# Six blocks of the last round sorted by pair of experts and run as 17 listed steps in place of 24

## The reference

```python
for r in range(R):                                # R = 4 rounds
    flat = cur.reshape(-1, h)
    logits = flat @ Wg[r] + bg[r]
    vals, idx = jax.lax.top_k(logits, TOPK)       # TOPK = 2 of E = 4
    w = jax.nn.softmax(vals, axis=-1)
    cw = jnp.sum(jax.nn.one_hot(idx, E, dtype=flat.dtype) * w[..., None], axis=1)
    hmid = jax.nn.gelu(jnp.einsum('nh,ehf->enf', flat, W1) + b1[:, None, :])
    y = jnp.einsum('enf,efh->enh', hmid, W2) + b2[:, None, :]
    cur = cur + jnp.einsum('ne,enh->nh', cw, y).reshape(b, s, h)
...
xn = _layernorm(x)
x = x + mixer(xn) * _silu(experts(xn))
```

## Time and profile before

| what | us |
|---|---|
| median of three runs | 784.72 |
| lowest and highest | 784.56, 784.82 |
| span of the profiled execution | 782.9 |
| TensorE busy in it | 777.2 |
| VectorE busy | 689.3 |
| ScalarE busy | 641.1 |
| GpSimd busy | 115.2 |

### The profile page before, as it was taken

One profiled execution on the slowest core, in us unless ns is written; L12 is line 12 of the kernel. 1 busy time (PEld: TensorE's weight loads), 2 busy tenths in 40 slices (PEclk: granted clock), 3 DMA queues, 4 the chain that ended last, 5 costly groups with the idle time before them and its releaser, 6 DMA issues.

```text
span 782.9 us, 9951 instructions
## 1 busy us (share of the span) xinstructions
PE 777.2 (99%) x3392; PEld 619.2 (79%) x3392; DVE 689.3 (88%) x1096; ACT 641.1 (82%) x873; POOL 115.2 (15%) x141
## 2 busy tenths in 40 slices
PE   8999999999999999999999999999999999999998
PEld 6778788887888878888788887888877788888887
DVE  7999987899888889879899788987988989988998
ACT  7989888787888877888788877887877878888886
POOL 0122111111111111111111111111111111111110
PEclk9999999999999999999999999999999999999999
DMA  8467572332642416333154322643227434655453
GB/s 267 139 132 182 128 208 50 95 95 41 148 89 62 107 28 163 92 64 88 33 157 107 81 57 41 149 108 96 41 41 175 108 56 107 134 123 122 70 117 71
DMA packets 77010, 81.62 MB, mean 104 GB/s; under 512 B 48800, under 2 KB 54688, under 8 KB 72992
## 3 DMA queue, kind: packets, MB, share of 16 engines
q0 software_dynamic: 18624, 34.61, 25.8%
q1 hardware_dynamic: 57920, 46.11, 19.5%
q10 hardware_dynamic: 416, 0.26, 0.1%
HBM read 41.91 MB, written 3.93 MB: 59 GB/s over the span
## 4 chain that ended last, share of the span: by engine, by line
PE 95%; ACT 2%; DVE 2%; issue 0%; DMA 0%; DVEq 0%
PE h_bank L1079 15%; PE h_bank L1080 15%; PE h_bank L1083 15%; PE y_bank L1152 15%; PE y_bank L1142 15%; PE y_bank L1140 14%; PE p_bank L1079 2%; PE p_bank L1083 2%; PE p_bank L1080 2%; PE r_bank L1189 1%; ACT g L465 1%; ACT g_hi L471 1%; DVE g_lo L759 0%; DMA cur<-in_x 0%; DVE stats L600 0%
## 5 line engine op out<-in xcount | busy, mean ns | idle before, releaser
L465 ACT ACTIVATE g<-h_bank,b_c 128x512 f32<-128x512 f32 x512 | 329.3, 682 | 77.8 <-PE h_bank L1083 77.0
L759 DVE TENSOR_TENSOR g_lo<-g,g_hi 128x1024 fp32r<-128x1024 f32 x256 | 310.0, 1222 | 72.8 <-ACT g_hi L471 71.2
L471 ACT ACTIVATE g_hi<-g 128x1024 fp32r<-128x1024 f32 x256 | 271.8, 1062 | 8.1
L415 POOL DMA_DIRECT2D cur<-tmp x126 | 110.6, 878 | 642.4 <-DVE tmp L773 544.1
L1079 PE MATMUL h_bank<-cur_hi,w_hi 128*128 128x512 f32 x512 | 202.9, 396 | 0.2 <-ACT cur_hi L513 0.2
L1083 PE MATMUL h_bank<-cur_lo,w_hi 128*128 128x512 f32 x512 | 202.2, 395 | 0.0
L1080 PE MATMUL h_bank<-cur_hi,w_lo 128*128 128x512 f32 x512 | 202.1, 395 | 0.0
L1140 PE MATMUL y_bank<-g_hi,w_hi 128*128 128x512 f32 x504 | 196.2, 393 | 0.0
L1142 PE MATMUL y_bank<-g_hi,w_lo 128*128 128x512 f32 x488 | 193.6, 397 | 0.0
L1152 PE MATMUL y_bank<-g_lo,w_hi 128*128 128x512 f32 x504 | 137.9, 395 | 0.1
L1079 PEld LDWEIGHTS h_bank<-cur_hi,w_hi 128*128 128x128 f32 x512 | 96.2, 188 | 26.6 <-issue 3.8
(11 more groups left out here) (153 smaller groups left out, 410.5 us busy)
## 6 DMA issues: line engine op xcount, KB each, us to landing
cur<-tmp POOLq DMA_DIRECT2D x126, 256.0 KB, 3.3
cw_b<-cw_scratch SPq DMA_DIRECT2D x31, 1024.0 KB, 5.2
xn_t<-cur SPq DMA_DIRECT2D x8, 256.0 KB, 3.1
cur<-in_x SPq DMA_DIRECT2D x7, 256.0 KB, 5.0
xr<-in_x SPq DMA_DIRECT2D x28, 64.0 KB, 3.4
out<-o SPq DMA_DIRECT2D x28, 64.0 KB, 2.1
xn_scratch<-o POOLq DMA_DIRECT2D x6, 256.0 KB, 3.0
xr<-xn_scratch SPq DMA_DIRECT2D x24, 64.0 KB, 2.5
```

Of the source, the lines that this page charges most:

```text
L415: pool.dma_start(cur[:, block_of(s // E)], tmp[:, s % SUMS, :], accum_op=ALU.add).then_inc(summed, DMA)
L465: nc.scalar.activation(g[:, gb, ft * BLK:(ft + 1) * BLK], hb[ft][:, :], ACT.Gelu_apprx_tanh, bias=b1_c[:, e * FT + ft:e * FT + ft + 1]).th ...
L471: nc.scalar.activation(g_hi[:, gb, h], g[:, gb, h], ACT.Copy).then_inc(g_hi_done, 1)
L759: nc.vector.tensor_tensor(g_lo[:, gb, h], g[:, gb, h], as_f32(g_hi[:, gb, h]), ALU.subtract).then_inc(g_lo_done, 1)
```

## The change

The last round is done otherwise for blocks 0 to 5. The two best experts of their 3072 tokens are found ahead of time, the tokens are sorted by their pair of experts (six pairs, in an order in which neighbours share an expert), and the sorted tokens are cut into six blocks again. A sorted block then needs only the experts of the pairs that lie in it. A list of block and expert is made on the chip; it always has 17 entries, and each is run as one step (an item) with its block, weights, bias and gate read through registers. If fewer are needed, the rest of the 17 run with a gate of zeros. Steps 0 to 95 are rounds 0 to 2, steps 96 to 99 block 6, steps 100 to 116 the items, steps 117 to 120 block 7. So there are 121 steps.

Around that:

- TensorE turns each of the six blocks to rows of tokens (`turn_row`, four transposes), counts the pairs (`count_pairs`), turns the sorted rows back (`turn_back`), turns the gates, and after the items turns each block to rows (`turn_end`). All of these go through the one bank `r_bank`, in a fixed order (`BANK_JOBS`).
- GpSimd scatters the rows to their places in `sorted_rows` (4 indirect DMAs for a block), gathers the mixer's result and x of the sorted tokens (4 for a block), and scatters the output rows (4 for a block).
- SyncE copies the expert's weights of each item from SBUF to SBUF into one of three places `staged` (two copies of 512 KB for an item), with bias and gate.
- VectorE finds pairs and places, makes the list (`list_items`, 20 small instructions), and multiplies and adds at the end (`silu_product`, `finish_rows`). For the sorted blocks these stand in place of the former end stages.
- The mixers of blocks 0 to 6 start every 11 steps instead of every 14, with 13 stages each; the projection of R moves into the stage of `mixer_values`, and the inverse root into that of `mixer_squares`. The last mixer runs in steps 102 to 114.
- `g_lo` lies in the same memory as `g`.

```diff
@@ -13,9 +13,13 @@
 TPB = BLK // D
 RP = 32
 RT = BLK // RP
-TURNS = R * NB
-STEPS = TURNS * E
-PASSES = TURNS // 2
+
+SORTED = 6
+ITEMS = 2 * SORTED + 5
+TURNS = R * NB - SORTED
+FIRST_ITEM = E * (TURNS - 1)
+LAST_AT = FIRST_ITEM + ITEMS
+STEPS = LAST_AT + E
 GRP, GW = 16, 8
 LN_EPS = 1e-5
...
-MIX_FROM, MIX_EVERY = 15, 14
-END_FROM = STEPS - E * NB + E
+MIX_AT = (15, 26, 37, 48, 59, 70, 81, 102)
+STAGES, PLACES = 13, 3
...
-JOB_AT = {0: J_W, 1: J_A, 2: J_K, 3: J_V, 5: J_R, 6: J_G, 12: J_S}
+JOB_AT = {0: J_W, 1: J_A, 2: J_K, 3: J_V, 4: J_R, 5: J_G, 10: J_S}
...
+def items_through(j):
+    return min(2 * j + 7, ITEMS)
...
+SORT_LOGITS_AT = {0: 80, 1: 89}
+COUNTS_AT = 89
+ROW_END, ROW_MID = {0: 84, 1: 85, 2: 86, 3: 91, 4: 92}, {5: 94}
+BACK_END, BACK_MID = {0: 97, 3: 99, 5: 100}, {1: 98, 2: 99, 4: 100}
+SILU_AT = {j: FIRST_ITEM + items_through(j) + 1 for j in range(SORTED)}
+GATHER_AFTER = {0: 103, 1: 108, 2: 105, 3: 110, 4: 112, 5: 114}
...
+        def unit_of_w1(i):
+            return max(2 * i - 1, 0)
+
+        def unit_of_w2(i):
+            return min(2 * i + 2, 2 * ITEMS - 1)
+
+        def place_free(engine, v):
+
+            u = v - PLACES
+            if u < 0:
+                return
+            if u == 2 * ITEMS - 1:
+                engine.wait_ge(down_done, LAST_AT)
+            elif u == 0 or u % 2 == 1:
+                engine.wait_ge(up_done, FT * (FIRST_ITEM + (u + 1) // 2 + 1))
+            else:
+                engine.wait_ge(down_done, FIRST_ITEM + (u - 2) // 2 + 1)
...
-                if k >= 2:
+                if k == TURNS - 1:
+                    sp.wait_ge(combined, 2 + FIRST_ITEM)
+                    sp.wait_ge(row_stored[2], DMA * TPB)
+                elif k >= 2:
...
+            def stage(v, src):
+
+                place_free(sp, v)
+                sp.dma_start(as_f32(staged[:, v % PLACES, :, :]), as_f32(src)).then_inc(stage_full[v % PLACES], DMA)
+
+            def stage_w1(i):
+                stage(unit_of_w1(i), w1_all[:, bass.ds(experts[i], 1), :, :].rearrange("p a n f -> p (a n) f"))
...
+                q = i % ITEM_PLACES
+                sp.wait_ge(combined, 2 + max(FIRST_ITEM - E, FIRST_ITEM + i - ITEM_PLACES + 1))
+                sp.dma_start(gate_item[:, q, :],
+                             sorted_gates[bass.ds(gate_rows[i], 1), :].rearrange("a c -> (a c)").partition_broadcast(128)).then_inc(gate_full[q], DMA)
...
+            def load_rows(j):
+
+                q = j % IN_PLACES
+                if j == 0:
+                    for n in range(OUT_PLACES):
+                        sp.wait_ge(row_sent[n], DMA * TPB * SORTED // OUT_PLACES)
+                if j >= IN_PLACES:
+                    sp.wait_ge(r_empty, bank_job("back", j - IN_PLACES) + 1)
+                    sp.wait_ge(tok_back, j - IN_PLACES + 1)
+                sp.dma_start(rows_in[:, q, :, :],
+                             sorted_rows[j * BLK:(j + 1) * BLK, :].rearrange("(t p) c -> p t c", p=128)).then_inc(row_back[q], DMA)
...
+
+            sp.wait_ge(listed, 1)
+            sp.wait_ge(b2_beside, 1)
+            regs = [sp.alloc_register(f"expert{n}") for n in range(ITEMS)]
...
+            stage_w1(0)
+            load_bias(0)
+            load_rows(0)
+            load_rows(1)
+            stage_w1(1)
+            load_bias(1)
...
+            load_rows(4)
+            stage_w2(1)
+            load_gate(1)
+            load_rows(5)
...
+            for i in range(3, ITEMS):
+                if i + 1 < ITEMS:
+                    stage_w1(i + 1)
+                    load_bias(i + 1)
+                stage_w2(i)
+                load_gate(i)
+                if i == 6:
+                    store(NB - 2)
+                    load_x_again(NB - 1)
+                elif i == ITEMS - 2:
+                    spread_gates(TURNS - 1)
...
+            def scatter_rows(j):
+
+                q = j % OUT_PLACES
+                pool.wait_ge(row_ready, j + 1)
+                pool.wait_ge(place_ready, 1)
+                for t in range(TPB):
+                    pool.indirect_dma_start(out=sorted_rows,
+                                            out_offset=bass.IndirectOffsetOnAxis(ap=place_i[:, j * TPB + t:j * TPB + t + 1], axis=0),
+                                            in_=rows_out[:, q, t, :], in_offset=None,
+                                            bounds_check=SORTED * BLK - 1).then_inc(row_sent[q], DMA)
...
+                else:
+                    pool.wait_ge(row_stored[j - 3], DMA * TPB)
+                for t in range(TPB):
+                    c = j * TPB + t
+                    pool.indirect_dma_start(out=s_and_x[j][:, t, :], out_offset=None, in_=sx_rows,
+                                            in_offset=bass.IndirectOffsetOnAxis(ap=id_i[:, c:c + 1], axis=0),
+                                            bounds_check=SORTED * BLK - 1).then_inc(sx_loaded[j], DMA)
+
+            def scatter_out(j):
+
+                pool.wait_ge(row_out, j + 1)
+                for t in range(TPB):
+                    c = j * TPB + t
+                    pool.indirect_dma_start(out=out, out_offset=bass.IndirectOffsetOnAxis(ap=id_i[:, c:c + 1], axis=0),
+                                            in_=s_and_x[j][:, t, 0:D], in_offset=None,
+                                            bounds_check=SORTED * BLK - 1).then_inc(row_stored[j], DMA)
...
+                else:
+                    pool.dma_start(cur[:, block_of(turn_of(s))], tmp[:, s % SUMS, :], accum_op=ALU.add).then_inc(summed, DMA)
+                if COUNTS_AT <= s < COUNTS_AT + SORTED:
+                    scatter_rows(s - COUNTS_AT)
+                for j in at_step(SILU_AT, s - 1):
+                    scatter_out(j)
+                for j in at_step(GATHER_AFTER, s):
+                    gather_sx(j)
...
+            def pair_tokens(half):
+
+                cols = COLS // 2
+                h = slice(half * cols, (half + 1) * cols)
+                rank_experts(bank_job("sort_logits", half), 128, cols, R - 1)
+                link(nc.vector.tensor_scalar(picked[:, h, :], rank[:, 0:cols * E].rearrange("p (t e) -> p t e", e=E), 1.5, None, ALU.is_lt))
+                for c, (a, b) in enumerate(PAIRS):
+                    last = nc.vector.tensor_tensor(pair[:, c, h], picked[:, h, a], picked[:, h, b], ALU.mult)
+                last.then_inc(pairs_set, 1)
+                score_experts(128, cols)
+
...
+            def silu_product(j):
+
+                dve.wait_ge(silu_th, j + 1)
+                nc.vector.scalar_tensor_tensor(out=silu, in0=silu, scalar=1.0, in1=cur[:, block_at(j)],
+                                               op0=ALU.add, op1=ALU.mult).then_inc(silu_ready, 1)
+
+            def finish_rows(j):
+
+                job, s_part, x_part = bank_job("end", j), s_and_x[j][:, :, 0:D], s_and_x[j][:, :, D:2 * D]
+                dve.wait_ge(sx_loaded[j], DMA * TPB)
+                dve.wait_ge(r_full, job + 1)
+                nc.vector.scalar_tensor_tensor(out=s_part, in0=rb[:, :].rearrange("p (t d) -> p t d", t=TPB), scalar=0.5, in1=s_part,
+                                               op0=ALU.mult, op1=ALU.mult).then_inc(r_empty, 1)
+                dve.wait_ge(r_empty, job + 1)
+                nc.vector.tensor_tensor(s_part, s_part, x_part, ALU.add).then_inc(row_out, 1)
...
+                        for j in at_step(SILU_AT, s - 1):
+                            finish_rows(j)
...
+                if s == COUNTS_AT:
+                    token_places()
+                elif s == BACK_END[5] + 1:
+                    token_ids()
+                for j in at_step(SILU_AT, s):
+                    silu_product(j)
...
+            def up_item(s1):
+
+                i = s1 - FIRST_ITEM
+                v, block = unit_of_w1(i), newest_block(i)
+                if i == 0:
+                    pe.wait_ge(listed, 1)
+                    regs = [pe.alloc_register(f"slot{n}") for n in range(ITEMS)]
+                    pe.load(regs, tables[0:1, T_SLOT, :])
+                    slots.extend(pe.snap(reg, donate=True, min_val=0, max_val=SPLITS - 1) for reg in regs)
+                hi, lo = (ap[:, bass.ds(slots[i], 1), :].rearrange("p a c -> p (a c)") for ap in (cur_hi, cur_lo))
+                w_hi, w_lo = w1_of(s1)
+                pe.wait_ge(stage_full[v % PLACES], DMA * (v // PLACES + 1))
+                pe.wait_ge(sorted_split, 2 * block + 1)
+                for ft in range(FT):
+                    pe.wait_ge(gelu_done, FT * (s1 - 1) + ft + 1)
+                    w = slice(ft * D, (ft + 1) * D)
+                    mm_high(hb[ft][:, :], w_hi[:, w], w_lo[:, w], hi)
+                    if ft == 0:
+                        pe.wait_ge(sorted_split, 2 * block + 2)
+                    mm_low(hb[ft][:, :], w_hi[:, w], lo).then_inc(up_done, 1)
...
+            def count_pairs():
+
+                pe.wait_ge(r_empty, bank_job("counts", 0))
+                pe.wait_ge(consts_made, 1)
+                pe.wait_ge(pairs_set, 2)
```

(18 more changed lines are left out.)

713 lines of the change are left out of this document (544 added, 169 removed).

## The result

The changed kernel takes **803.3 us** (median; 803.0 to 804.1), the kernel before 784.7 in the same comparison: 1.024 times as long, 95% interval 1.0225 to 1.0254. So it is slower by 2.4%, where 772 and faster was forecast. The profiled execution has a span of 801.3, against 782.9.

The account below looks back on a forecast made before the run. TensorE, busy 99% of the span, was taken as the bound: 28.6 us less work, less the waits, gave -12.3 against 782.9, so 770.6, and 772 with the 1.8 around it; range 764 to 780, chance 0.60.

Parts of the forecast that it names:

- Sum: -28.6 + 7.1 + 0.5 + 2.7 + 1.0 + 5.0: TensorE's work, VectorE's lateness, `turn_back(0)`, `turn_back(5)`, register load and last item's weights, in us: -12.3 in all.
- VectorE, steps 47, 82, 106: VectorE's carried-over work makes TensorE wait 0.5, 1.0 and 0.2 us in these steps.
- `count_pairs`: Step 89: squares, root, `g_lo` and ranking on VectorE make `pair` late; TensorE waits 3.0 us.
- `silu_product` at `turn_end`: Near step 110: VectorE delivers the product late for `turn_end`; one wait of 2.4 us.
- `turn_back(0)`: End of step 97: sorted rows arrive after scatters and SyncE's register loads; nothing to 2.6 us, taken as 0.5.
- `turn_back(5)`: Step 100: `load_rows(5)` stands behind `stage_w2(1)` on SyncE's queue; wait of 2.7 us (0 to 4).
- registers, first item: TensorE's register load ahead of the first item costs 1.0 us, taken from a round trip of 1.7.
- end of SyncE's queue: Step 116: `stage_w2(16)` comes behind `spread_gates(25)` and its 1 MB, so `down(116)` waits 5.0 us (2 to 8).
- step 110: VectorE's squares, root, a split and carry 3.3 make `silu_product` late for `turn_end`: 2.4 us.
- Register loads cost by the register: Rival: at 0.21 us each, 3.6 on TensorE and 2.1 more at `turn_back(0)`: 777 us; chance 0.12.
- GpSimd becomes the bound: Rival: indirect DMAs of 1.7 us delay steps 89 to 94 and 108 to 115: 791.5 us; chance 0.06.
- The third rival: Copies of weights come late in each item, steps 100 to 116, 14 waits of 0.9: 785 us; chance 0.07.

Follow-up runs that it names:

- a_fill: The changed kernel with TensorE given transposes of the identity to do in seven of its long waits; 803.9 us.
- a_late: The changed kernel with block 2's rows in `xn_t`, `turn_end` of blocks 0 to 4 behind the `down`, output scatters and gathers of blocks 3 to 5 a step later; 805.6 us.
- a_early: The changed kernel with gathers of blocks 2, 3 and 4 in free memory of `xn_t`, issued earlier without waiting for output scatters; 794.6 us.
- a_plain_out: The changed kernel with one plain DMA per block for each four indirect ones of the s and x gathers and output scatters, rows not reordered; 795.5 us.
- a_pad128: The changed kernel with 128 unused bytes per partition ahead of `cur_hi`; 810.1 us.

## Why the prediction was wrong

**Step that failed: the sizes of the waits.** "Sum: -28.6 + 7.1 + 0.5 + 2.7 + 1.0 + 5.0" gives TensorE 16.3 us of waits. The trace has 36.4. That is 20.1 of the 30.7 us by which the span (801.3) missed the 770.6 of the prediction. The costs behind them are in the next part: a block of scatters takes 6.5 us of GpSimd and not 5.3, a load of 17 registers 4.2 and not 1.0, the last copy of weights waits for everything ahead of it.

**Step that was missing: the sum had no term for what a wait leaves behind**, and none for the end of the kernel. It prices each wait at its own length. The trace shows 47 matmuls at half clock behind the waits, 9.4 us, 8.5 more at the edges, and 4.7 behind the last matmul. a_fill shows that the half clock comes from the waits, but not that mending it gives the time back. In the profile of before TensorE never waits more than 0.5 us after its start and the clock has no dip, so no row could show it there. The Trainium skill tells that the chip halves TensorE's clock when it has had too little to do ("TensorE: Matmul & The Clock Gate", section "Part 1: The HAM clock gate (the "warmup" mystery)"); the trace agrees, with 0.43 against 0.23 us.

**The waits, by place.** The mechanisms were right in all but two, the sizes were not:

| term | predicted | measured |
|---|---|---|
| VectorE, steps 47, 82, 106 | 0.5, 1.0, 0.2 | 0.6, 1.4, 0.7 |
| `count_pairs` | 3.0 | 4.2 |
| `silu_product` at `turn_end` | 2.4, once | 6.6, four times |
| `turn_back(0)` | 0.5 | 3.2 |
| `turn_back(5)` | 2.7 | 3.6 |
| registers, first item | 1.0 | 2.6 (a load of 4.2) |
| end of SyncE's queue | 5.0 | 8.4 |
| ScalarE behind an accumulate | none | 2.9 |
| gates of round 1 behind six copies | none | 0.4 (up to 3.3 in other runs) |

- VectorE: "step 110" gave the one wait for `silu_product` that I priced. The profile has it at `turn_end` of blocks 0, 1 and 3 (2.5, 1.9, 1.7) and a small one at the end: the product stands at the end of a step on VectorE, behind `combine`, and is asked for in the middle of the next.
- `turn_back(0)`: "the scatters end late in step 96". They ended late in step 97 (611.2), because a block takes 6.5 us of GpSimd, not 5.3. The price of an indirect DMA was right (1.04 against 1.1); the 0.30 ahead of each was left out.
- Registers: the rival *Register loads cost by the register* came near on TensorE, 0.25 each, where the earlier trace rows gave 0.21. It is not the whole rule, since SyncE's second load of 17 took 1.22. The Trainium skill's rule ("Runtime: NRT & Kernel Launch", section "Instruction fetch mechanics"), about 200 ns a register, would give an estimate of 3.4 us for either: 4.22 and 1.22 were measured, and the measurements decide. SyncE's 34 were hidden behind the scatters.
- End of SyncE's queue: right in kind, late by the same lateness of GpSimd that I had priced at 1.1 per DMA.
- The rival *GpSimd becomes the bound* came nearest in its sign and total (791.5), at a lower price than "from about 1.5 us on": 1.04 and 0.30 make 1.34, and it takes no buffer of `tmp` to pass the lateness on, since `silu_tanh` waits for the accumulate directly. I had looked for `combine` as the one who waits. a_late, a_early and a_plain_out show it. That a gather waits until an earlier output scatter has landed (1.74, in a_late 6.64) I had counted for the last gates alone, not for the accumulates behind it.
- The third rival (copies of weights late in item after item) holds for two or three items only when something else is taken away.

**The pace of the matmuls** was taken as a constant ("0.23 us between matmuls as now"). It changed by 3%, some 14 us of work less, and hid part of the loss. That was luck, since nothing in the change aimed at it. Without it the time is 810.1 (a_pad128), 6.8 more.

**Why the gain did not come**, in a sentence: 42.6 us of work and pace were freed, and about 59 were put back, 36.4 in waits, 17.9 at half clock and its edges, 4.7 at the end, because each of the three short queues (GpSimd's, VectorE's in step 89, SyncE's last items) was fuller than TensorE's.

## What to carry to other kernels

Where TensorE is at 99%, taking 4% of its work away only helps if every other queue has as much to spare in that very stretch; count an issue gap with each DMA of GpSimd, and ask of each engine, ScalarE too, what it stands in front of when it waits. Ask what a wait of TensorE leaves behind: here 36.4 us of waits had 9.4 of half clock behind them, 17.9 with the edges. But filling the waits did not shorten the kernel, so shorten the waits. Before tuning a schedule, try the start of the moving tensors at a few offsets: it is one line, and here it was worth more than the whole change.

## What I had not expected of the hardware

- Where the tensors start changes TensorE's pace: with `cur_hi`, `g_hi` and `g_lo` at 64 and 128 modulo 256 bytes a matmul of 512 columns in a step takes 0.233 us, at 192 0.227; the kernel of 128 steps takes 784.7, 785.7 and 771.3, and 774.2 at 0. The projections do not follow this order. Whether it is the start of what TensorE reads, its distance to the weights or what the other engines write beside it was not taken apart.
- A second load of 17 registers on SyncE, right behind the first, took 1.22 us against 4.15. Why is open.
- Ahead of each indirect DMA on GpSimd stands a gap of 0.30 us; ahead of an accumulate that follows one directly there is none.
- In several runs one step of the first two rounds (10, 17 or 18) was up to 4 us longer in the profiled execution than in others, at the first use of a transfer of gates; so single edits worth under 3 us could not be told apart here by time, only by the profile.
